# Edge stage of a graph kernel: first group of one-hot matrices built among the marks, shorter lead of the sums, 16-bit ids

## The reference, cut to what matters

```
x = x + _L0_gnn_ref(_layernorm(x), edge_index, W_e, W_r, a)      # 10000 edges, 8 heads of 64
    h_e, h_r = einsum('nf,hfd->hnd', x, W_e), einsum('nf,hfd->hnd', x, W_r)
    diff  = h_r[:, dst] - h_r[:, src]
    score = s_src + s_dst + diff.a_dif + abs(diff).a_abs + (h_r[src]*h_r[dst]).a_prd
    alpha = leaky_relu(score)
    att   = exp(alpha - max over src) / sum over src
    out   = segment_sum(att * h_e[:, dst], src)
```

## Time and profile before

| | us |
|---|---|
| median of 3 runs | 2372.29 (2369.41 to 2374.41) |
| the profiled execution | 2365.97 |
| its span, first to last instruction | 2364.1 |
| busy: TensorE matmul, weight load | 2167.1 (92%), 1251.0 (53%) |
| busy: VectorE, ScalarE, GpSimd | 1045.1 (44%), 728.2 (31%), 556.0 (24%) |

### The profile page before, as it was taken

The page is one execution under the profiler, slowest core; times in us unless marked ns, Lnnn a source line. Parts: engine busy times, 40 slices in busy tenths (PEclk is TensorE's granted clock), DMA queues, the critical chain, the costliest instruction groups (busy, mean ns, idle before and its releaser), DMA issues.

```text
span 2364.1 us, 21963 instructions
## 1 busy us (share of the span) xinstructions
PE 2167.1 (92%) x8167; PEld 1251.0 (53%) x8167; DVE 1045.1 (44%) x2140; ACT 728.2 (31%) x1221; POOL 556.0 (24%) x469
## 2 busy tenths in 40 slices
PE   5799875788899999997899999999999999999998
PEld 3477553676544654543455555555555544444443
DVE  8798664689333333335535445445344410000002
ACT  1377552677322120002234233233233111111110
POOL 3677752344211010001201201201101110022202
PEclk9899888789799979998899999999999899999999
DMA  9532233330120110004101101101101467777732
GB/s 373 133 65 48 46 83 84 88 86 1 56 87 25 54 54 20 0 1 182 64 14 54 64 13 54 66 11 54 58 1 54 166 247 306 293 295 303 293 154 70
DMA packets 61475, 243.33 MB, mean 103 GB/s; under 512 B 23183, under 2 KB 25699, under 8 KB 39244
## 3 DMA queue, kind: packets, MB, share of 16 engines
q1 hardware_dynamic: 31866, 174.12, 20.5%
q0 software_dynamic: 26336, 62.19, 8.7%
q10 hardware_dynamic: 3168, 5.63, 0.7%
HBM read 209.96 MB, written 31.92 MB: 102 GB/s over the span
## 4 chain that ended last, share of the span: by engine, by line
PE 67%; DVE 10%; issue 10%; PEld 4%; DMA 3%; POOL 3%; ACT 3%; SPq 0%; PEldq 0%; ACTq 0%; DVEq 0%; POOLq 0%
PE PS L710 10%; PE PS L982 10%; PE PS L703 7%; PE PS L1374 6%; PE PS L1383 6%; PE PS L1412 6%; PE PS L853 3%; PE PS L1280 3%; PE PS L1020 2%; PE PS L1260 2%; POOL pair_scores L1956 2%; PE PS L721 1%; PEld PS L703 1%; DMA pair_scores<-TS,SIDX 1%; DVE AR L2377 1%
## 5 line engine op out<-in xcount | busy, mean ns | idle before, releaser
L1927 POOL TENSOR_TENSOR RSTD<-VE,HALF 125x1 f32<-125x1 f32 x100 | 82.1, 821 | 1026.6 <-DVE VE L2089 1026.6
L853 PE MATMUL PS<-HR,HOT 125*125 125x512 f32 x800 | 215.8, 418 | 32.6 <-DVE HOT L2234 32.6
L982 PE MATMUL PS<-XT,WR 128*128 128x500 f32 (+2 forms) x992 | 233.3, 392 | 8.5 <-ACT XT L1480 4.4
L710 PE MATMUL PS<-WR,XT 128*125 128x512 f32 (+1 forms) x464 | 210.2, 601 | 13.2 <-DVE AR L2665 6.8
L2880 DVE TENSOR_TENSOR AR<-AR,PS 128x512 f32<-128x512 f32 (+1 forms) x44 | 30.3, 688 | 405.0 <-PE PS L1383 405.0
L982 PEld LDWEIGHTS PS<-XT,WR 128*128 128x128 f32 x992 | 144.7, 193 | 88.1 <-issue 72.7
L853 PEld LDWEIGHTS PS<-HR,HOT 125*125 125x125 f32 x800 | 150.0, 196 | 75.3 <-DVE HOT L2234 24.9
L1945 POOL DMA_INDIRECT pair_sums<-CW,SIDX x80 | 133.3, 1666 | 55.2 <-DMA pair_sums<-CW,SIDX 22.9
L710 PEld LDWEIGHTS PS<-WR,XT 128*125 128x125 f32 x464 | 88.2, 197 | 103.8 <-issue 87.7
L703 PE MATMUL PS<-XT,WR 128*128 128x113 f32 (+3 forms) x432 | 126.5, 450 | 2.0 <-DVE CW L2195 1.5
L2111 DVE TENSOR_TENSOR AR<-PS,AR 125x512 f32<-125x512 f32 x55 | 38.0, 691 | 189.0 <-PE PS L710 106.2
(11 more groups left out here) (411 smaller groups left out, 3974.0 us busy)
## 6 DMA issues: line engine op xcount, KB each, us to landing
WR<-in_qkv SPq DMA_DIRECT2D x12, 1024.0 KB
WR<-in_omm SPq DMA_DIRECT2D x12, 1024.0 KB
pair_scores<-CNT SPq DMA_DIRECT2D x1, 12212.0 KB
AR<-pair_scores SPq DMA_DIRECT2D x5, 2187.5 KB
AR<-in_x_a SPq DMA_DIRECT2D x10, 1024.0 KB, 9.3
AR<-in_x_b SPq DMA_DIRECT2D x10, 1024.0 KB, 4.9
AR<-in_x_c SPq DMA_DIRECT2D x10, 1024.0 KB, 7.0
WR<-in_x_a SPq DMA_DIRECT2D x8, 1024.0 KB, 9.0
```

What stands on the lines that cost most here:

```text
L710: last = mm(s.ap[0:P, 0:cols], lhs, rhs, start=(k == 0), stop=(k == len(pairs) - 1))
L853: last = mm(DIFF[m % 4], HOT[g % 2][0:P, k, tile(j)], HR[0:P, k, :, b, :], start=(k == 0 and b == 0), stop=(k == NT - 1 and b == 1))
L982: last = mm(by_tile(s)[:, t0:t1, :], w[:, k, 128 * m:128 * (m + 1)], XT[:, k, P * t0:P * t1].rearrange("p (c n) -> p c n", n=P), start=(k ...
L1927: g.tensor_tensor(RSTD[:, t:t + 1], VE[:, t:t + 1], HALF[:, :], ALU.pow)\
```

## The change

LEAD becomes 20. The ids are written once as 16-bit numbers: VectorE casts them (two casts ahead of the keys), SyncE stores them to a small table `short_ids` and waits for it to land before it loads the first ids and clears `pair_scores`; IDB is loaded from that table in 16 bits. The factors (PRODUCT) are computed ahead of the projections, the node rows ahead of the last projection. The first group's HOT (parts 0 to 4) goes to the other of the two buffers, which doesn't overlap the marks; ScalarE builds its `apart` and `from_hot` between its copies of HE, VectorE builds `hot(0)` to `hot(3)` before the last `total` and `hot(4)` after it.

```diff
-LEAD = 24
+LEAD = 20
-ROWS_FILL = STEPS // 2 + 1
+ROWS_FILL = STEPS // 2
+    short_ids = nc.dram_tensor("short_ids", [2, E], I16, kind="Internal").ap()
-        HOT = [HOT0, HOT1]
-        IDB = [view(12696 + 2000 * b, 128, 2, 1000, dt=I32) for b in range(2)]
+        HOT = [HOT1, HOT0]
+        IDB = [view(12696 + 1000 * b, 128, 2, 1000, dt=I16) for b in range(2)]
+        SHORT_IDS = THIRD[0:ET, 1344:1344 + P].bitcast(I16).rearrange("p (a b) -> p a b", a=2)
 SyncE
             def edge_ids(j):
-                for r, name in enumerate(("src_p", "dst_p")):
-                    ids = a[name].rearrange("p e -> (p e)")
-                    sp.dma_start(IDB[j % 2][:, r, :], bcast(ids, 1000 * j, 1000, 128))\
+                for r in range(2):
+                    sp.dma_start(IDB[j % 2][:, r, :], bcast(short_ids[r], 1000 * j, 1000, 128))\
                       .then_inc(ids_in[j % 2], 16)
...
+            sp.wait_ge(short_ids_ready, 1)
+            for r in range(2):
+                sp.dma_start(short_ids[r].rearrange("(m q) -> m q", q=P), SHORT_IDS[:, r, :])\
+                  .then_inc(short_ids_out, 16)
+            sp.wait_ge(short_ids_out, 32)
             edge_ids(0)
             edge_ids(1)
 TensorE
+            s = fill("N")
+            pe.wait_ge(arow_in, 96)
+            for h in range(HEADS0):
+                last = mm(s.ap[:, h:h + 1], TWICE[:, 128 * h:128 * (h + 1)], ONES[0:1, 0:1],
+                          start=True, stop=True)
+            last.then_inc(s.filled, 1)
             weights(0, 2)
...
                 before = marked
+                if i == STEPS - 1:
+                    pe.wait_ge(uv_ready, 1)
+                    rows = fill("W")
+                    wide(rows, 96, K4, lambda k: V3[:, k, :], lambda k: XT[:, k, :])
+                    rows_at = n.now(rows.filled)
                 project_narrow(wr if i < NT else we, i % NT)
             totals(STEPS - 1, before)
 (the same lines are gone from behind the loop)
 ScalarE
+            act.wait_ge(start_done, 9)
+            act.wait_ge(keys_ready, 2)
+            for t in range(NT):
+                if t == NT - 1:
+                    psum.skip(T=ET // 4, W=STEPS - 1)
+                    s = take("W")
+                    fn(NODE_ROWS, s.ap[0:96, 0:N], ACT.Copy)
+                    fn(VROW[:, :], s.ap[0:96, 0:N], ACT.Copy).then_inc(s.taken, 1)
+                    act.wait_ge(s.taken, n.now(s.filled))
+                    psum.skip(W=1)
+                s = take("N")
+                fn(HE[:, t, :], s.ap[0:P, :], ACT.Copy).then_inc(s.taken, 1)
+                if t < 4:
+                    apart(t)
+                    from_hot(t)
+            apart(4)
+            from_hot(4)
...
             act.wait_ge(weights_used, 1)
-            apart(0)
+            apart(NT)
...
-                    if q + 1 < NT * GROUPS:
+                    if NT < q + 1 < NT * GROUPS:
                         apart(q + 1)
-                    from_hot(q)
+                    if g:
+                        from_hot(q)
 VectorE
             dve.wait_ge(index_in, 48)
+            v.tensor_copy(SHORT_IDS[:, 0, :], SRC_ROWS)
+            v.tensor_copy(SHORT_IDS[:, 1, :], DST_ROWS).then_inc(short_ids_ready, 1)
...
-            total(STEPS - 1)
-            psum.skip(N=NT + 2, W=1)
...
+            dve.wait_ge(hr_split, NT)
+            v.memset(ZB, 0.0)
+            for k in range(4):
+                hot(k)
+            psum.skip(W=1)
+            total(STEPS - 1)
+            hot(4)
+            psum.skip(N=NT + 1)
...
-                if g < GROUPS:
+                if 0 < g < GROUPS:
                     for k in ks:
                         hot(NT * g + k)
```

More of the change, by code:

```diff
@@ L418, in program @@
         terms_ready, row_part_ready = sem("terms_ready"), sem("row_part_ready")
+        short_ids_ready, short_ids_out = sem("short_ids_ready"), sem("short_ids_out")
         ids_in = [sem(f"edge_ids_in_{b}") for b in range(2)]
@@ L1491, in _ @@
             transpose_y()
+            s = take("N")
+            fn(PRODUCT[:, :], s.ap[:, 0:HEADS0], ACT.Copy).then_inc(s.taken, 1)
             for t in range(NT):
@@ L1495, in _ @@
                 fn(Y[0:P, t, :], s.ap[0:P, :], ACT.Copy).then_inc(s.taken, 1)
[L1496 to L1510, removed]
             def apart(q):
@@ L1527, in from_hot @@
                 fn(FROM[q % 4], APART[q % 4], ACT.Relu, bias=1.0, scale=-1.0).then_inc(from_ready, 1)
+            act.wait_ge(start_done, 9)
[8 more added lines that the diff above has]
+                    psum.skip(W=1)
+                s = take("N")
+                fn(HE[:, t, :], s.ap[0:P, :], ACT.Copy).then_inc(s.taken, 1)
[4 more added lines that the diff above has]
+            from_hot(4)
+            s = take("N")
+            fn(U[:, :, :], s.ap[0:P, 0:16 * NT].rearrange("p (t c) -> p t c", t=NT)[:, :, 8:16], ACT.Copy)\
+                .then_inc(s.taken, 1)
+            act.wait_ge(s.taken, n.now(s.filled))
+            act.wait_ge(uv_ready, 1)
             def magnitude(m):
@@ L1535, in magnitude @@
                 fn(Z[m % 4], DIFF[m % 4], ACT.Abs).then_inc(diff_taken, 1)
-            act.wait_ge(start_done, 9)
             act.wait_ge(weights_used, 1)
-            apart(0)
+            apart(NT)
             for g in range(GROUPS):
@@ L2209, in node_terms @@
                 v.tensor_tensor(V3[:, :, 8:16], part[0], part[1], ALU.subtract).then_inc(uv_ready, 1)
+            psum.skip(N=1)
             for i in range(STEPS):
@@ L2284, in _ @@
                 v.memset(S2[b][:, :, 64:65], 1.0)
-            v.memset(ZB, 0.0)
             def merge(t):
@@ L2298, in _ @@
                 if g == 1:
-                    dve.wait_ge(slots["W"][STEPS % 2].taken, ROWS_FILL)
+                    dve.wait_ge(slots["W"][(STEPS - 1) % 2].taken, ROWS_FILL)
                     v.tensor_tensor(REST, NODE_ROWS, VROW[:, :], ALU.subtract).then_inc(uv_ready, 1)
```

## The result

The changed kernel takes 2360.45 us in the median of 10 runs (2352.73 to 2362.72), the kernel before beside it 2372.38 (2368.21 to 2375.56, 10 runs). The ratio is 0.9947, 95% interval 0.9934 to 0.9959: 12.6 us faster, between 9.7 and 15.7. The forecast was 2358.5, and -13.8 us.

What follows compares the result with a forecast made beforehand. GpSimd's puts and sums were taken to pace the edge stage. Start of put 0 -10.8, LEAD 20 +4.1 and 16-bit ids -7.1 made -13.8 us: 2358.5 against 2372.3, own range 2353 to 2362, with rivals 2351 to 2369.

Steps and rivals of the forecast that it cites:

- What bounds the stage: Edge stage: GpSimd's puts and sums pace it, TensorE and VectorE are held by the ring; an undisturbed pair takes 3.43 us.
- Start of put 0, -10.8: GpSimd's first put goes out at 108.5 instead of 119.33 us, behind sum 20 (108.2) and score 0 (108.4).
- LEAD 20, +4.1: GpSimd's edge stage: 59 pairs and 20 single puts replace 55 and 24, costing 4.1 us.
- 16-bit ids, -7.1: Puts beside id loads: landing stalls go with the bytes, so 14.2 us of them halve, saving 7.1 us.
- the five stalls at the loads of the sums: Among the puts alone: five are held 3 to 5 us by loads of the sums, and this stays.
- second rival: Puts beside id loads: the stall hangs on packets, not bytes; total -6.7 us, 2365.6 us; chance 0.11.
- first rival: Puts beside id loads: the stalls vanish altogether, -12 us; total -18.7 us, 2353.6 us; chance 0.12.
- HOT on 16-bit ids, 0: VectorE's HOT: one input of 2 bytes, output still 4, so the same duration, 0.74 us; effect 0.
- Rival 5: VectorE's HOT on 16-bit ids holds GpSimd's issue in the pairs: net +13.6 us, 2386 us; chance 0.05.
- The merge: VectorE's wait for the sums at the first merge stays hidden: score 63 is ready 5 us before its put.
- rival 4: After TensorE's 25 us pause at the first merge, 12 differences stay at low clock: +14 us, 2372 us; chance 0.04.
- rival 3: Put 0 hardly moves, early sums slipping or ScalarE's chain longer: at 115, total -7.3 us; at 119, -3.3; chance 0.10.

Runs made afterwards that it cites:

- late_first_group: The changed kernel with the first group's one-hot matrices built behind the marks as before, in that group's own buffer; 2364.7 us, ratio 0.9978 to the kernel before.
- lead_20_alone: The kernel before with LEAD 20 in place of 24 and nothing else of the change; 2375.3 us, ratio 1.0015.
- lead_24: The changed kernel with LEAD back at 24; 2364.2 us, ratio 0.9971 to the kernel before.
- ids_16_alone: The kernel before with the 16-bit ids alone (casts, table, SyncE's wait), LEAD still 24; 2364.5 us, ratio 0.9978.
- changed_again: The changed kernel run once more with no edit; 2358.5 us, ratio 0.9941 to the kernel before.
- ids_one_row: The changed kernel with source and destination ids side by side, each load one DMA of 4000 bytes a partition instead of two of 2000; 2349.1 us, ratio 0.9904.
- one_row_again: ids_one_row repeated in a later group of runs; 2351.5 us, ratio 0.9917 to the kernel before.
- lead_16: The changed kernel with LEAD 16 in place of 20; 2363.8 us, ratio 0.9964 to the kernel before.
- no_later_ids: The changed kernel with id loads 2 to 9 left out, so later groups use the first ones' ids; 2348.2 us, ratio 0.9897 to the kernel before.
- one_row_lead_19: ids_one_row with LEAD 19 in place of 20; 2349.3 us, ratio 0.9905 to the kernel before.
- ids_32_bit: The changed kernel with the ids loaded in 32 bits again, without casts or table; 2362.3 us, ratio 0.9947 to the kernel before.

## Why the prediction was right, point by point

**What bounds the stage.** Right, and shown: every kernel above has pairs of 3.39 to 3.43 us once the waits are taken out, whatever TensorE and VectorE did. What follows put 79 keeps its length to 0.1 us in the two profiles compared; that it does so this closely is luck, since the second profile of the changed kernel has it 5.7 us longer.

**Start of put 0, -10.8.** Measured -10.66, and -8.9 between the second profiles of the two kernels. The total is right, its halves less so. I had score 0 at 108.4 and sum 20's end at 108.2 (the rows give 107.8, and the working doesn't say where the other 0.4 comes from). Score 0 came at 106.29: the first difference at 96.10 instead of 97.5, because the marks ran 1.1 to 1.2 us earlier than I took them from the earlier trace rows (node rows at 85.37, not 86.5; in the profiles of this family they start anywhere from 83.8 to 86.7, so this is partly chance), and the chain from there to score 0 took 10.2 us, not 10.9. So score 0 is there before sum 20's end, and the sums alone hold put 0. My premise that TensorE's clock would not fall there did not hold: it was granted 0.71 and 0.72 from 96 to 102 us (last section), and the first four differences took 11.10 us. late_first_group shows that the mechanism, TensorE's 9.5 us idle behind the matrices, was the right one. Of the up to 2 us that I had feared for the early sums 0.8 came: sum 20 went out at 106.81 instead of 105.99.

**LEAD 20, +4.1.** The pairs gave 4 x 3.40 = +13.6 and the puts alone -12.17, of which 4 x 2.485 = 9.94 are the four puts (2.485 is the mean of the 19 steps of before that no load of the sums holds). That makes +3.7 for the lead; lead_20_alone gave +3.6, with an interval from -0.7 to +7.8. Behind sum 24, put 0 would have been 7.4 us later by my count; lead_24 measured 8.6.

**16-bit ids, -7.1.** Between the two profiles this is the term that came out short: -3.8 us among the pairs (15.7 to 11.9), where about 8 us of waits were to be left. It shows in sum 79 too, at 319.34 instead of the 316 forecast. The comparison mixes two things, though. With its ids in 32 bits the changed kernel waits 19.8 us, so there the ids bring 8, and the earlier start with its new lead had added 4 which the sum had not; lead_20_alone, with 15.7, shows that it is not the lead by itself. The size of -7.1 is thus borne out by the waits of both pairs of kernels that differ in the ids alone (-7.5 to -8.4), and by the times only within wide bounds (ids_16_alone -5.2, from -9.0 to -1.4).

Another 2.2 us came off the five stalls at the loads of the sums, which I had said would stay (30.4 instead of 32.6 us of put intervals). That is luck: the 20 puts alone took 67.7 us here, 68.8 in changed_again and up to 72.3 in the other kernels with a lead of 20. It is what brought the total so near.

The step that failed is that the stall goes with the bytes and nothing else: at equal bytes ids_one_row and one_row_again wait 3.4 and 5.6 us instead of 11.4 to 11.9. My second rival, a stall that hangs on packets alone (0 for this term), fails as well, since 16 bits took off waiting at an equal number of packets. The estimate of -3.6 us by the Trainium skill ("DMA: Bandwidth & Descriptors", Anatomy of one DMA) is nearest to the -3.8, and its 4.3 us that become 3.2 are near the flows measured, 4.1 and 3.3. The same sum over bytes has no term for packets, by which ids_one_row differs and is faster. I took the flow's end from the earlier trace rows and halved it; the flow fell by a fifth, while the waits fell by 40 to 50%. My first rival, stalls that vanish for -12, nearly came true with one DMA of 128 packets in place of two with 256.

**HOT on 16-bit ids, 0.** Right: 732 ns in the mean against 733, and GpSimd's means are unchanged. Rival 5 is dead.

**The merge.** Right, 5 us forecast and 4.9 found; lead_16 shows what stands behind it (13.77 us), and TensorE's pause of 22.4 us cost one slow difference (4.63 us, against 4.36 in the earlier trace rows), so rival 4 is dead too:

```profile
337.57 4.63 PE L861 MATMUL PS<-HR,HOT 125*125 125x512 f32 x10 [22.43 <-DVE HOT L2249]
```

**Signs.** Pairs over 3.6 us were to be a sign against me; they took 212.53/59 = 3.602, a hair over it, because less waiting was gone than I had said. No put alone waited for a score by more than 0.5 us over an ordinary landing, put 0 moved in full (rival 3 falls), and the time is inside the forecast's own range. That it is within 2 us of the forecast is partly luck, as the terms above show.

## What to carry to other kernels

Where one queue issues in a written order, write its time as start, pairs and singles, and ask of each edit which of the three it moves: a shorter lead was +3.6 us alone (not clear of 0) and -5.7 us behind an earlier first score. When transfers stall something small beside them, count their packets and DMAs as well as their bytes: two arrays that are read together belong in one row and one load, which here took off about as much waiting again as halving the element size. Before shortening a lead further, look for the place late in the stage where the same lead pays for a merge.

## What the runs showed of the hardware

**Packets.** 0.51 MB broadcast to 128 partitions flowed in 2.8 to 4.0 us (3.3 in the mean of 17) as two DMAs of 2000-byte packets and in 2.2 to 2.8 us (2.5 in the mean of 13) as one of 4000-byte packets, beside the same kind of scatters. 1.02 MB as two DMAs of 4000-byte packets took 4.1 us in the mean of 16.

**TensorE's clock moves its low stretch.** It falls to the low level (0.50 of full speed, 1.2 of 2.4 GHz) somewhere between 82 and 102 us in each profile of the changed kernel's family but late_first_group, and not always in the same place. A value between 0.50 and 1 is a stretch with both levels in it. Busy time by stretch, columns as in the earlier trace rows, first of the changed kernel, then of one_row_again:

```profile
96.00:99.00 3.00, 2.90 (x9) 2.35 (x10) 0.86 (x3) 2.02 (x6) 2.33 (x3) 0.71 0.35 43
99.00:102.00 3.00, 3.00 (x11) 2.33 (x10) 2.04 (x4) 3.00 (x7) 2.69 (x2) 0.72 0.25 9
```

```profile
86.00:89.00 3.00, 2.71 (x4) 1.03 (x5) 2.96 (x11) 0.00 (x0) 0.00 (x0) 0.50 1.05 404
89.00:92.00 3.00, 3.00 (x5) 1.06 (x4) 2.68 (x8) 0.00 (x0) 1.47 (x1) 0.50 0.73 257
```

In the first the node rows take 4.42 us and the 40 matmuls of the first four differences 11.10; in the second 7.30 and 9.48. The second form costs 2.9 ahead of the last projection and gives 1.6 back. The long node rows are seen in no_later_ids, one_row_again, one_row_lead_19, lead_24 and changed_again (in ids_32_bit both are long, 5.91 and 11.04), and in the first three of these put 0 waits 2.5 us for score 0, at 109.28 to 110.97. What decides between the two was not tried. It is why a put 0 that differs by 2 or 3 us between single profiles says nothing of an edit behind it.
